# A gated graph layer with its biases in the weights, its rows and scaling on ScalarE, and a new order on every engine

## The reference

```python
in_degrees = jnp.sum(adj, axis=-1)
norm = jnp.power(in_degrees + 1e-06, -0.5)[..., None]
f_hom = jnp.einsum('bnd,de->bne', x, theta) * norm
f_hom = jnp.einsum('bnm,bmd->bnd', adj, f_hom) * norm
f_het = jnp.einsum('bnd,de->bne', x, W_h)
gate = jax.nn.sigmoid(jnp.einsum('bnd,de->bne', x, W_t) + b_t)
out = gate * f_hom + (1.0 - gate) * f_het
return jax.nn.elu(out)          # added to the input of the layer
```

## Time and profile before

| | |
|---|---|
| median of 3 runs | 3868.84 us (3862.88 to 3871.17) |
| the profiled execution | 3861.43 us, span 3859.7 us |
| mean granted TensorE clock | 0.885 |
| TensorE busy | 2905.4 us, 75% |
| VectorE busy | 2249.4 us, 58% |
| ScalarE busy | 1547.1 us, 40% |
| GpSimd busy | 939.9 us, 24% |
| the changed stage | from 966 us to about 1253 us of the span |

### The profile page before, as it was taken

How to read it: one execution, slowest core, us unless ns; L and a number is a source line. 1 busy time by engine, 2 the same in 40 slices (tenths; PEclk the granted TensorE clock), 3 DMA queues, 4 the chain that set the end, 5 groups by cost and what they waited for, 6 DMA issues and landing times. The chain is left out here.

```text
span 3859.7 us, 66559 instructions
## 1 busy us (share of the span) xinstructions
PE 2905.4 (75%) x18192; PEld 2100.5 (54%) x18193; DVE 2249.4 (58%) x6435; ACT 1547.1 (40%) x4549; POOL 939.9 (24%) x922
## 2 busy tenths in 40 slices
PE   4999957881675791669999999688885777739991
PEld 3666634550565571536666666456553444427771
DVE  5555532335686346467677777388884677623333
ACT  1333313442222222634444444266663555414442
POOL 0222333441134131511111111000001133323331
PEclk9999979995777895789999999799997888859996
DMA  4101102223211111400000000000001000011114
GB/s 152 34 33 33 35 31 60 66 66 113 101 49 39 47 53 49 146 4 1 1 0 0 0 0 1 19 18 22 22 17 47 12 19 20 23 35 55 55 55 142
DMA packets 164806, 161.76 MB, mean 42 GB/s; under 512 B 19664, under 2 KB 150736, under 8 KB 164048
## 3 DMA queue, kind: packets, MB, share of 16 engines
q1 hardware_dynamic: 143184, 115.60, 10.0%
q0 software_dynamic: 21504, 44.74, 3.3%
HBM read 109.21 MB, written 51.05 MB: 42 GB/s over the span
## 5 line engine op out<-in xcount | busy, mean ns | idle before, releaser
L1032 POOL DMA_INDIRECT y_rows<-ffn_e_rows_out,ffn_e_scatter_at x352 | 337.9, 960 | 584.0 <-DVE ffn_e_rows_out L1066 365.9
L802 POOL DMA_INDIRECT sorted_rows<-ffn_r_h,ffn_r_slot x320 | 312.8, 978 | 262.0 <-issue 262.0
L1081 DVE TENSOR_TENSOR ffn_e_hid<-ffn_e_act,bank 128x256 f32<-128x256 f32 (+1 forms) x280 | 130.2, 465 | 414.4 <-ACT ffn_e_act L1117 414.4
L1165 PE MATMUL bank<-constants,ffn_e_hidT 128*128 x1968 | 277.5, 275 | 0.5 <-issue 0.4
L1147 PE MATMUL bank<-constants,ffn_e_xT 128*128 x432 | 230.7, 616 | 42.1 <-issue 23.3
L1117 ACT ACTIVATE ffn_e_act<-bank 128x256 f32<-128x256 f32 (+1 forms) x280 | 117.5, 420 | 339.9 <-PE bank L1145 181.2
L1165 PEld LDWEIGHTS bank<-constants,ffn_e_hidT 128*128 128x128 f32 x1968 | 247.3, 191 | 1.1 <-issue 1.0
L1108 ACT ACTIVATE ffn_e_hidT<-bank 128x256 f32<-128x256 f32 (+2 forms) x352 | 163.8, 465 | 146.8 <-PE bank L1155 146.8
L2337 ACT ACTIVATE gnn_prob<-bank,gnn_low 128x256 f32<-128x256 f32 x512 | 193.9, 490 | 51.9 <-DVE gnn_low L2255 51.9
L2255 DVE TENSOR_REDUCE gnn_low<-bank 128x2 f32<-128x512 f32 x256 | 159.0, 684 | 62.8 <-PE bank L2431 62.7
L1155 PEld LDWEIGHTS bank<-ident,ffn_e_hid 128*128 128x128 f32 x984 | 126.8, 141 | 114.1 <-issue 66.8
(11 more groups left out here) (480 smaller groups left out, 7105.7 us busy)
## 6 DMA issues: line engine op xcount, KB each, us to landing
g_adj<-in_adjT SPq DMA_DIRECT2D x48, 512.0 KB, 4.0
ffn_e_rows_in<-sorted_rows SPq DMA_DIRECT2D x352, 66.0 KB, 1.8
ffn_c_y<-y_rows SPq DMA_DIRECT2D x80, 256.0 KB, 2.9
gnn_adj<-in_adjT SPq DMA_DIRECT2D x16, 512.0 KB, 4.0
constants<-in_ffn SPq DMA_DIRECT2D x1, 6741.0 KB, 19.7
constants<-in_ffn SPq DMA_DIRECT2D x1, 6281.0 KB, 17.7
y_rows<-ffn_e_rows_out,ffn_e_scatter_at POOLq DMA_INDIRECT x352, 2.2
constants<-in_ffn SPq DMA_DIRECT2D x1, 5206.0 KB, 15.2
```

The costliest lines, as they stand in the source:

```text
L802: g.indirect_dma_start(self.c.sorted_rows, bass.IndirectOffsetOnAxis(self.slot[par][:, k, j:j + 1], 0), self.h[par][:, j, :], None).then_i ...
L1032: g.indirect_dma_start(c.y_rows, bass.IndirectOffsetOnAxis(scatter_at[par][:, k:k + 1], 0), rows_out[par][:, k, :], None).then_inc(scatter ...
L1081: v.tensor_tensor(hid[k][:, 0:m.hidden], act[k % 2][:], up, ALU.mult).then_inc(hid_ready, 1)
L1165: ins = pe.matmul(B[6 + par][:, k * D:(k + 1) * D], hidT[k % 2][:, ch * P:(ch + 1) * P], weights, start=(ch == 0), stop=(ch == NCH - 1))
```

## The change

**Biases in the weights.** A normalised row adds up to zero, so its last feature is minus the sum of the others. The change puts a 1 there (`h[:, :, D-1:D]` is set once), takes the last row of each weight off all its rows, and puts the gate's bias in the last row of w_t. It makes the new weights `fused` once at the start: one product with `differ` (identity less a matrix of ones in the last row), then three VectorE operations. The gate's bias add is gone, and ScalarE reads the gate's product from PSUM with its tanh.

**ScalarE.** It makes the normalised rows (`rows_h`, 127 features) and the scaled theta product (`f`), and also relu of the mixed value. Per turn its order is: copy of the transposed rows of t+1; routing rows of t-1; `front(t+1)`, that is four scalings, tanh, copy of het; exp and relu of t; the routing's transposed rows and exp of t-1; `rows_h(t+2)`.

**Elu.** It is formed as min(exp(v), 1) + relu(v) - 1 by two VectorE operations that add straight into `c.X`; `c.xs` and its copy are not used. `mixed` goes to SBUF in two buffers, not to bank 6.

**Order on VectorE.** `degrees(t+1)` stands ahead of L1369's operation; the routing's choice of t-1 stands between the mixed value and the X update, its gates behind the row statistics.

**Order on TensorE.** A turn opens with the transposes and degrees of t+1, then rank of t-2, then the aggregation of t, then the three weights of t+1, then the routing's transposes and logits.

The core of the diff:

```diff
@@ vector, in turn() @@
+                    if not last:
+                        degrees(t + 1)
-                    v.wait_ge(agg_ps, t + 1)
-                    v.wait_ge(het_ready, t + 1)
+                    v.wait_ge(agg_ps, now)
+                    v.wait_ge(het_ready, now)
                     for k in range(TT):
                         ins = v.scalar_tensor_tensor(diff[:, k, :], B[5][:, k * P:(k + 1) * P], norm[par][:, k:k + 1],
                                                      het[par][:, k, :], ALU.mult, ALU.subtract)
-                    then(v, ins, diff_ready, t + 1)
-
-                    v.wait_ge(gate_ready, t + 1)
-                    g6 = tiles4(B[6][:])
-                    then(v, v.scalar_tensor_tensor(g6, g6, 1.0, diff[:], ALU.add, ALU.mult), scaled, t + 1)
-                    then(v, v.scalar_tensor_tensor(g6, g6, 0.5, het[par][:], ALU.mult, ALU.add), mixed, t + 1)
-
-                    v.tensor_scalar(pos[:], B[6][:], 0.0, None, ALU.max)
-                    v.tensor_scalar(neg[:], B[6][:], 0.0, None, ALU.min).then_inc(neg_ready, 1)
-                    v.wait_ge(exp_ready, t + 1)
-                    then(v, v.scalar_tensor_tensor(ex[:], ex[:], -1.0, pos[:], ALU.add, ALU.add), elu_ready, t + 1)
-                    then(v, v.tensor_tensor(c.xs[:], tiles4(ex[:]), c.X[:, ds(t * TT, TT), :], ALU.add), x_sum, t + 1)
-                    finish_rows(v, c, t).then_inc(route.rows_in, 1)
-                    if not last:
-                        front(t + 1, 1 - par)
-                    if not (isinstance(t, int) and t >= TURNS - 2):
-                        normalised(t + 2)
+                    then(v, ins, below, now)
+                    v.wait_ge(gate_ready, now)
+                    then(v, v.scalar_tensor_tensor(diff[:], gate[par][:], 1.0, diff[:], ALU.add, ALU.mult), scaled, now)
+                    v.scalar_tensor_tensor(mixed[par][:], diff[:], 0.5, het[par][:], ALU.mult, ALU.add).then_inc(mixed_ready, 1)
                     if not first:
                         route.vector_first(v, t - 1, 1 - par, before)
                         route.vector_chosen(v, t - 1, before)
+
+                    v.wait_ge(exp_ready, now)
+                    v.scalar_tensor_tensor(c.X[:, rows_, :], ex[:], 1.0, c.X[:, rows_, :], ALU.min, ALU.add).then_inc(x_sum, 1)
+                    v.wait_ge(x_sum, 2 * t + 1)
+                    v.scalar_tensor_tensor(c.X[:, rows_, :], pos[:], -1.0, c.X[:, rows_, :], ALU.add, ALU.add).then_inc(x_sum, 1)
+                    v.wait_ge(x_sum, 2 * t + 2)
+                    for k in range(TT):
+                        at = ds(t * TT + k, 1)
+                        ins = v.bn_stats(c.ST[:, at, :], c.X[:, at, :])
+                    ins.then_inc(route.rows_in, 1)
+                    if not first:
                         route.vector_gates(v, t - 1, before)
@@ scalar @@
+                def rows_h(t):
+                    wait_past(a, hT_ps, t)
+                    for k in range(TT):
+                        at = ds(t * TT + k, 1)
+                        ins = a.activation(h[:, k:k + 1, 0:D - 1], c.X[:, at, 0:D - 1], ACT.Identity, bias=c.shift[:, at], scale=c.rstd[:, at])
+                    ins.then_inc(h_ready, 1)
...
-                def evac_het(t, par):
+                def front(t, par):
+                    a.wait_ge(norm_ready, t + 1)
+                    a.wait_ge(f_ps, t + 1)
+                    for k in range(TT):
+                        ins = a.activation(f[par][:, k, :], B[1][:, k * P:(k + 1) * P], ACT.Copy, scale=norm[par][:, k:k + 1])
+                    ins.then_inc(f_ready, 1)
+                    a.wait_ge(gate_ps, t + 1)
+                    a.activation(gate[par][:], tiles4(B[2][:]), ACT.Tanh, scale=0.5).then_inc(gate_ready, 1)
                     a.wait_ge(het_ps, t + 1)
                     a.activation(het[par][:], tiles4(B[3][:]), ACT.Copy).then_inc(het_ready, 1)
...
                 def turn(t, par, first, last):
-                    a.wait_ge(gpre_ready, t + 1)
-                    wait_past(a, neg_ready, t)
-                    a.activation(B[6][:], gpre[par][:].rearrange("p k d -> p (k d)"), ACT.Tanh, scale=0.5).then_inc(gate_ready, 1)
                     if not last:
                         evac_hT(t + 1, 1 - par)
                     if not first:
                         route.scalar_rows(a, t - 1, 1 - par)
-                    a.wait_ge(neg_ready, t + 1)
-                    a.activation(ex[:], neg[:], ACT.Exp).then_inc(exp_ready, 1)
                     if not last:
-                        evac_het(t + 1, 1 - par)
+                        front(t + 1, 1 - par)
+                    a.wait_ge(mixed_ready, t + 1)
+                    wait_past(a, x_sum, 2 * t)
+                    a.activation(ex[:], mixed[par][:], ACT.Exp)
+                    a.activation(pos[:], mixed[par][:], ACT.Relu).then_inc(exp_ready, 1)
                     if not first:
                         route.scalar_hT(a, t - 1)
                         route.scalar_exp(a, t - 1)
+                    if not (isinstance(t, int) and t >= TURNS - 2):
+                        rows_h(t + 2)
@@ tensor @@
+                pe.wait_ge(differ_ready, 1)
+                mm(B[5][:, 0:3 * D], differ[:], W[:, 0:3 * D], start=True, stop=True).then_inc(fused_ps, 1)
+                degrees(0, 0)
+                to_features(0)
+                pe.wait_ge(fused_ready, 1)
                 front(0, 0)
 
                 def turn(t, par, first, last):
+                    if not last:
+                        to_features(t + 1)
+                        degrees(t + 1, 1 - par)
+                    if not first and not (isinstance(t, int) and t == 1):
+                        route.tensor_rank(pe, t - 2)
                     pe.wait_ge(f_ready, t + 1)
-                    wait_past(pe, diff_ready, t)
+                    wait_past(pe, below, t)
...
                     ins.then_inc(agg_ps, 1)
-                    if not first and not (isinstance(t, int) and t == 1):
-                        route.tensor_rank(pe, t - 2)
                     if not last:
                         front(t + 1, 1 - par)
```

More of the change, by code:

```diff
@@ L1283, in phase_gnn1 @@
         adj = [sb(f"adj{i}", [P, 4, NODES]) for i in range(2)]
-        one = sb("one", [P, 1])
+        one, ones, differ, fused = sb("one", [P, 1]), sb("ones", [P, P]), sb("differ", [P, P]), sb("fused", [P, 3, D])
         deg = sb("deg", [P, TT])
@@ L1287, in phase_gnn1 @@
         f = [sb(f"f{i}", [P, TT, D]) for i in range(2)]
-        gpre = [sb(f"gpre{i}", [P, TT, D]) for i in range(2)]
         het = [sb(f"het{i}", [P, TT, D]) for i in range(2)]
-        diff, neg, pos, ex = sb("diff", [P, TT, D]), sb("neg", [P, TURN]), sb("pos", [P, TURN]), sb("ex", [P, TURN])
-        one_ready = sem("one_ready")
+        gate = [sb(f"gate{i}", [P, TT, D]) for i in range(2)]
+        mixed = [sb(f"mixed{i}", [P, TT, D]) for i in range(2)]
+        diff, ex, pos = sb("diff", [P, TT, D]), sb("ex", [P, TT, D]), sb("pos", [P, TT, D])
+        one_ready, differ_ready, fused_ps, fused_ready = sem("one_ready"), sem("differ_ready"), sem("fused_ps"), sem("fused_ready")
         adj_ready = [sem(f"adj_ready{i}") for i in range(2)]
@@ L1295, in phase_gnn1 @@
         deg_ps, deg_ready, norm_ready = sem("deg_ps"), sem("deg_ready"), sem("norm_ready")
[L1296 to L1300, removed]
+        f_ps, f_ready, gate_ps, gate_ready, het_ps, het_ready = sem("f_ps"), sem("f_ready"), sem("gate_ps"), sem("gate_ready"), sem("het_ps"), sem("het_ready")
+        agg_ps, scaled, mixed_ready = sem("agg_ps"), sem("scaled"), sem("mixed_ready")
+        exp_ready, below, x_sum = sem("exp_ready"), sem("below"), sem("x_sum")
         route = Route(nc, c, "ffn1", c.moe, ctx, B[4], B[4], B[4])
@@ L1333, in _, with degrees @@
             def _(v):
-                v.memset(one[:], 1.0).then_inc(one_ready, 1)
-                def front(t, par):
+                v.memset(h[:, :, D - 1:D], 1.0)
+                v.memset(ones[:], 1.0)
+                then(v, v.memset(one[:], 1.0), one_ready, 1)
+                then(v, v.tensor_scalar(ones[:], ones[:], last_row, None, ALU.mult), one_ready, 2)
+                v.tensor_tensor(differ[:], c.ident[:], ones[:], ALU.subtract).then_inc(differ_ready, 1)
+                v.wait_ge(fused_ps, 1)
+                weights = B[5][:, 0:3 * D].rearrange("p (k d) -> p k d", k=3)
+                v.tensor_copy(fused[:, 0, :], weights[:, 0, :])
+                v.tensor_copy(fused[:, 2, :], weights[:, 2, :])
+                v.scalar_tensor_tensor(fused[:, 1, :], w["b_t"], last_row, weights[:, 1, :], ALU.mult, ALU.add).then_inc(fused_ready, 1)
+                def degrees(t):
                     v.wait_ge(deg_ps, t + 1)
@@ L1339, in front @@
                     v.tensor_scalar(deg[:], B[7][:, 0:TT], 1e-6, None, ALU.add).then_inc(deg_ready, 1)
[L1340 to L1353, removed]
-                normalised(1)
+                degrees(0)
```

(4 more changed lines are left out.)

12 lines of the change are left out of this document (7 added, 5 removed).

## The result

The changed kernel takes 3884.54 us (median of five, 3878.47 to 3889.04) against 3862.88 us for the kernel before beside it (median of five, 3857.93 to 3871.17): ratio 1.0051 over all executions (the two medians alone would give 1.0056), 95% interval 1.0036 to 1.0065. That is slower by about 20 us.

A forecast was written before the change was run, and what follows sets the result against it. VectorE had least slack before; after, a closed logits-to-logits chain with cold degrees and aggregation takes 16.9 us a turn. Start, thirteen turns (219.7) and an 18.0 us tail give 19 us more: 3888 us, range 3857 to 3905.

The forecast's parts named there:

- What VectorE loses: VectorE in the gated graph layer: the change takes away about 4.5 to 5.5 us of work in a 15.88 us turn.
- The chain: Gated graph layer: one turn is a closed loop from logits to logits through three engines, 16.9 against 15.88 us.
- tanh and het: ScalarE's tanh and copy of het behind the scaling: 0.54 and 0.48 us from start to start, sum 14.2.
- The unseen costs: ScalarE steps without a row: scaling out of PSUM 1.2 us, upper end 1.65; relu 0.48 to 0.54; no table reload.
- rival D: Relu or scaling from PSUM dearer, or logits cold: 0.5 to 1 us more a turn, 3895 to 3910; chance 0.11.
- The clock: TensorE: degrees and aggregation stay at the low clock, which rises near the aggregation's end; bounds, turn 16.1 to 17.6 us.
- B: TensorE's degrees warm the array, so rank, aggregation and theta run high: turn 15.2 us, time 3864; chance 0.17.
- C: TensorE's clock never falls, its idle times being short: loop closes in 13.9 us, time 3843; chance 0.12.
- Start and tail: Graph layer's ends: first aggregation ends near 997, first logits at 1018, tail 18.0 us; L667's point 19 us later.

The follow-up runs named there:

- narrow filler: Changed kernel plus fourteen useless one-column TensorE products a turn, 6 ahead of the transposes and 8 ahead of the logits: 4101.97 us, ratio 1.0056.
- wide filler: Changed kernel plus fourteen useless 128-column TensorE products a turn, 6 ahead of the transposes and 8 ahead of the logits: 4067.13 us, ratio 0.9958.
- all three edits: Changed kernel with TensorE's order of before, rows of t+2 early on ScalarE and the routing's first choice late on VectorE: 3844.94 us, ratio 0.9937.

## Why the prediction was right

**The size.** Forecast +19 us on the profiled execution (+0.49%), 3888 us; measured ratio 1.0051, 3884.54 us, and +23.1 us on the profiled execution.

**What VectorE loses.** Predicted 4.5 to 5.5 us a turn. Busy time a turn went from 154.73 / 190.20 of 15.88, which is 12.9, to 96.70 / 11 = 8.8 us: 4.1 less, a little under the range. A part of the gap is the row statistics, four in 1.00 or 1.11 us where the old line took 0.86. It didn't matter, as predicted.

**The chain.** By steps in the turn above, predicted and measured: L695 to routing exp 0.67, 0.68 (L695 stood at 1135.11 - 17.10 = 1118.01); exp 0.23, 0.22; rows 1.65, 1.78; transposes 0.89, 0.90; degrees 3.27, 3.27; rank and aggregation 4.16, 4.09; theta 1.1, 1.17; scaling 1.2, 1.01; tanh and het 1.02, 1.21; exp and relu 1.04, 1.04; hT 0.59, 0.64; logits 1.06, 1.09. Sums 16.9 and 17.1. The largest miss, tanh and het, has a cause that the chain hadn't: the copy of het waits for the last weight, whose products end at 1128.95 + 2.85 = 1131.80, and starts at 1131.84. TensorE and not ScalarE was last at that one point. `mixed` ends at 1131.74, 0.6 ahead of exp; I had 0.7.

**The unseen costs.** Four scalings from PSUM to the next operation's start, 1.01 us against a taken 1.2, bounded by 1.65; exp to relu to hT at 0.52 each; one table load in the stage. The groups of ScalarE in the stage:

```profile
L1415 ACT ACTIVATE g_f<-bank,g_norm 128x128 f32<-128x128 f32 x64 | 18.3, 368 | 24.0 <-PE bank L1473 24.0
...
L1436 ACT ACTIVATE g_pos<-g_mixed 128x512 f32<-128x512 f32 x15 | 9.3, 618 | 0.0
L1435 ACT ACT_TABLE_LOAD x1 | 1.3, 1283 | 0.0
```

So rival D's dearer relu or scaling didn't come, nor did its cold logits, 1.06 us in steady turns. The Trainium skill, ScalarE: Activation LUTs (What ACT_TABLE_LOAD costs), gives an operation 186 ns plus 0.833 per element, 93 more for a pointer operand, and an overlap of 93 with its neighbour; the estimate from it is a start every 0.29 us, and the trace has 0.25 (1.01 / 4).

**The clock.** Degrees and aggregation at 0.50, high only as the aggregation ends: this was the step of the forecast most open to doubt, and it held from 1005.72 on: eleven steady aggregations took 3.73 to 3.76 us, and their degrees 3.41. The turn that it was read from, with degrees cold at 1068.27, is the only such one among the twelve steady turns of before; in the others they took 1.84 to 2.09 us behind an aggregation that ran cold. So the forecast's reading, that the clock came back behind an aggregation and not within the degrees, fits those turns too, but the prediction didn't say how rare its row was. Rivals B and C are out: no steady aggregation ran at 2.0 us, and narrow filler didn't bring that about while wide filler did. Had C come, its turn would not have been 13.9 us by its own terms: 7.1 and the 5.9 from theta to logits are 13.0, and the turns with wide filler in which both ran fast took 13.5. The Trainium skill, TensorE: Matmul & The Clock Gate (What's actually happening), says that the hardware doesn't count instructions and that whatever work is issued runs at 1.2 GHz at first and at 2.4 GHz behind that. Here TensorE works without a gap from 1120.69 to 1128.95, through transposes, degrees, rank and aggregation, with the clock still at 0.50 in the window to 1128.90, and the two filler kernels differ in the products' width alone. Both disagree with the page; the measurement decides.

**Start and tail.** What failed, and only by size, was the start: the forecast put the first aggregation's end 3.8 us behind that of before (993.2), and it came 1.0 behind. The degrees ahead of it took 1.84 us; it ran at the high clock and ended at 994.2, not 997, the second at 1009.5 and not 1012.2, and the first logits were in at 1015.5, not 1018. Thirteen turns, to the logits' end at 1237.44, took 221.9 us and not 219.7, and the tail to L667 (at 1254.04) 16.6 and not 18.0. Together L667 came 17.4 us later than before, with 19 predicted: 2.5 us early at the start, 2.2 late over the turns and 1.4 early in the tail. These misses cancel in part, and so far the nearness of the sum is luck. The profiled execution was 23.1 us longer and not 19, since 5.7 us arose outside the stage, a part for which no step of mine stood; the ratio of all executions, some 20 us, is nearer to the forecast than either.

**What stays open.** Why the clock falls behind the degrees in some turns and not in others. The steady turns of the changed kernel are all between 17.01 and 17.16 us and those of before between 15.5 and 16.6; that goes with degrees that are cold in every turn of the one and in one turn (1068.27) of the other, but what sets it wasn't tried. Nor was the cause of the 5.7 us outside the stage.

## What to carry to other kernels

Taking a third of the busiest engine's work away gained nothing here, because the order closed a loop through three engines: follow one turn from a point back to the same point, add up starts, and compare that with the measured turn, before you sum anyone's busy time. A slow piece of work, cold or not, that had slack can be moved onto the loop by putting it behind something else in an in-order queue; here undoing either of two such moves brought a gain of the same size, and undoing both no more. Test such a theory by opening the loop at two places in turn.

## What the hardware showed that I had not expected

- The granted clock can fall while TensorE is at work without a gap: 1.00 over transposes and degrees (1093.40 to 1095.50, busy 2.10 of 2.10), 0.57 over the 2.50 us of 128-column weights right behind them.
- Narrow and wide filler left a different clock behind them. Filler at 1.00 with 1.30 of 1.30 us busy, then some 1.3 us idle, had the degrees at 0.50 when it was 1 column wide; with 128 columns and 1.2 us idle they ran at 1.00, and at 0.50 only in the two turns with 2.1 us idle.
- Work that nobody reads can pay: eight products a turn took the turn from 13.66 to 12.78 us and the ratio from 0.9916 to 0.9889 (intervals overlapping), and in the kernel with all three edits the turn from 13.55 to 13.24 us and the ratio from 0.9937 to 0.9896. The stage ended 11.0 and 7.7 us earlier.
- Row statistics, four 128x128 BATCH_NORM_STATS2, took 1.00 or 1.11 us on `c.X` in the turns of the loop, where a running index addresses it, and 0.87 in the turns written out; 0.86 before the change on `c.xs`. That the index is the cause is argued, not shown.
